# Float32r scores in row halves of the array, read two banks at a time

## The reference

```python
scores = jnp.einsum('bhqd,bhkd->bhqk', q, k) / math.sqrt(Hd)
scores = scores + causal[None, None]
attn = jax.nn.softmax(scores, axis=-1)
out = jnp.einsum('bhqk,bhkd->bhqd', attn, v)
```

## Time and profile before

| | us |
|---|---|
| median of 3 runs (782.05 to 785.3) | 783.87 |
| span of the profiled execution | 782.6 |
| stage 0 to 80: norm, first projections, first maxima | 80 |
| stage 80 to 512: maxima and scores together | 432 |
| stage 512 to 600: scores without maxima, with the work put beside them | 88 |
| stage 600 to 783: routing and experts | 183 |

### The profile page before, as it was taken

How to read it: one execution, slowest core, us unless ns; L and a number is a source line. 1 busy time by engine, 2 the same in 40 slices (tenths; PEclk the granted TensorE clock), 3 DMA queues, 4 the chain that set the end, 5 groups by cost and what they waited for, 6 DMA issues and landing times.

```text
span 782.6 us, 12208 instructions
## 1 busy us (share of the span) xinstructions
PE 689.1 (88%) x4290; PEld 367.2 (47%) x4290; DVE 561.1 (72%) x1467; ACT 459.5 (59%) x962; POOL 133.9 (17%) x194
## 2 busy tenths in 40 slices
PE   4686989999999998999999999989996279999994
PEld 3564534432323343323332323242543269999994
DVE  7754778788888787988888898960435437777762
ACT  1422445566676667766677676657783336656551
POOL 6000222220001132003310201100105300121122
PEclk9869889999999999999999999999999559999998
DMA  7436126630006033005900006000004283455200
GB/s 243 109 76 144 41 57 147 162 68 14 2 0 162 1 81 81 2 1 124 308 1 1 1 1 214 1 28 1 28 28 162 90 234 115 155 182 201 92 23 17
DMA packets 42111, 66.53 MB, mean 85 GB/s; under 512 B 3822, under 2 KB 31985, under 8 KB 41466
## 3 DMA queue, kind: packets, MB, share of 16 engines
q1 hardware_dynamic: 39746, 59.44, 27.3%
q0 software_dynamic: 2304, 6.31, 2.2%
HBM read 39.36 MB, written 26.78 MB: 85 GB/s over the span
## 4 chain that ended last, share of the span: by engine, by line
PE 74%; DVE 10%; ACT 8%; issue 4%; DMA 2%; POOL 1%; SPq 0%; DVEq 0%; POOLq 0%; ACTq 0%
PE bank L1245 17%; PE bank L1295 15%; PE bank L1325 14%; PE bank L1430 9%; PE bank L1413 8%; ACT probs L802 4%; PE bank L1187 3%; DVE chunk_max L1049 2%; PE bank L1350 2%; PE bank L1216 1%; PE bank L1396 1%; ACT qk_sb L751 1%; PE bank L1373 1%; PE bank L1228 1%; DVE stats L907 1%
## 5 line engine op out<-in xcount | busy, mean ns | idle before, releaser
L802 ACT ACTIVATE probs<-bank 128x512 f32<-128x512 f32 (+3 forms) x640 | 298.3, 537 | 124.1 <-PE bank L1325 123.0
L1049 DVE TENSOR_REDUCE chunk_max<-bank 128x1 f32<-128x512 f32 x384 | 250.7, 685 | 36.9 <-PE bank L1295 35.9
L1325 PE MATMUL bank<-stacks 104*128 104x512 bf16 (+3 forms) x640 | 195.4, 356 | 13.5 <-ACT probs L802 10.1
L1295 PE MATMUL bank<-stacks 96*128 96x512 bf16 (+3 forms) x640 | 197.7, 359 | 7.9 <-DVE chunk_max L1049 3.2
L1245 PE MATMUL bank<-probs,v_sb 128*32 128x512 f32 (+3 forms) x1280 | 151.6, 546 | 0.1
L1055 DVE CUSTOM_DVE_ANT_0 masked<-bank,causal 128x128 bf16<-128x128 f32 (+3 forms) x256 | 120.7, 484 | 15.4 <-PE bank L1295 14.6
L1295 PEld LDWEIGHTS bank<-stacks 96*128 96x128 bf16 x640 | 56.0, 98 | 160.0 <-DVE chunk_max L1049 79.4
L698 POOL TENSOR_SCALAR_AFFINE_SELECT probs<-probs 128x512 f32<-128x512 f32 x64 | 40.6, 635 | 397.4 <-ACT probs L802 397.4
L1325 PEld LDWEIGHTS bank<-stacks 104*128 104x128 bf16 x640 | 62.2, 100 | 98.7 <-ACT probs L802 65.6
L1430 PE MATMUL bank<-w_split,acts 128*128 128x256 f32 x576 | 79.9, 284 | 0.0
L1430 PEld LDWEIGHTS bank<-w_split,acts 128*128 128x128 f32 x576 | 74.5, 190 | 1.5 <-issue 0.8
(11 more groups left out here) (140 smaller groups left out, 533.6 us busy)
## 6 DMA issues: line engine op xcount, KB each, us to landing
stacks<-qk_rows SPq DMA_DIRECT2D x6, 1536.0 KB, 12.4
w_raw<-w_in SPq DMA_DIRECT2D x8, 1024.0 KB, 5.0
w_raw<-w_down SPq DMA_DIRECT2D x8, 1024.0 KB, 8.0
qk_rows<-part SPq DMA_DIRECT2D x32, 192.0 KB, 2.9
slot_rows<-empty SPq DMA_DIRECT2D x1, 5140.0 KB, 28.9
slots_sb<-slot_rows SPq DMA_DIRECT2D x8, 514.0 KB, 4.0
qk_rows<-part SPq DMA_DIRECT2D x32, 128.0 KB, 2.4
stacks<-qk_rows SPq DMA_DIRECT2D x8, 384.0 KB, 4.5
```

Of the source, the lines that this page charges most:

```text
L802: act.activation(probs[:, s % 3, h, 0:width], bank[SCORE_BANKS[u % 3]][:, 0:width], ACT.Exp)\
L1049: dve.tensor_reduce(to, src[:, 0:QB], AX.X, ALU.max).then_inc(max_read, 1)
L1295: pe.matmul(bank[MAX_BANKS[u % 3]][:, 0:width], stack(g, 0)[0:KR, h, q0:q0 + P], stack(g, 1)[0:KR, h, c * QB:c * QB + width], start=True, ...
L1325: pe.matmul(bank[SCORE_BANKS[u % 3]][:, 0:QB - lo], stack(g, 1)[0:KR + MR, h, kt * P:(kt + 1) * P], stack(g, 0)[0:KR + MR, h, b * QB + lo: ...
```

## The change

1. The parts of q and k become two float32r parts in place of three bfloat16 ones. A head takes 3 x 16 = 48 rows (high x high, high x low, low x high) and 2 more for the maxima. Two heads stand side by side in the rows of the array: one in partitions 0 to 49, one in 64 to 113.
2. A unit is now two heads: two matmuls on the two row halves, into the two banks of a pair. There are 320 units of maxima and 320 of scores. One VectorE reduction and one ScalarE exponential read both banks.
3. The three pairs of banks serve maxima and scores alike; the plan says which unit takes which pair. In the last group, once no maxima are left, the work put beside the scores has pair 0 and the scores have the other two.
4. On the diagonal, TensorE adds the mask: four matmuls of 64 columns in bfloat16 (a matrix of the large negative number by an identity) are accumulated onto the last 128 columns of the unit. The masking read on VectorE is gone.
5. The splitting is two ScalarE reads of the projection and one subtraction per block; the selector rows of L780 are gone, rows of ones are placed by four DMAs. The row of maxima goes from ScalarE through SBUF and two DMAs of SP into the stack, in place of a copy by ScalarE and one by VectorE. SP now follows the plan, so that loading of the experts comes after the last block's rows.
6. The planner is rewritten: it goes by the unit that can start first. The maxima of block 0 all use pair 0.

```diff
-PARTS_Q = [0, 0, 0, 1, 1, 2]
-PARTS_K = [0, 1, 2, 0, 1, 0]
-KR = HD * len(PARTS_Q)
-MR = 2 * HG
+HALF = P // 2
+RUNS = 3
+KR = HD * RUNS
+MR = 2
...
+        while self.maxima[self.maxed][:2] == (0, 0):
+            self.emit_max(pair=0)
...
-        MAX_BANKS, SCORE_BANKS, VALUE_BANK, MISC_BANK = (0, 1, 2), (3, 4, 5), 6, 7
+        pairs = [ctx.enter_context(nc.psum_tensor(f"pair{i}", [P, 2, QB], F32)) for i in range(3)]
...
-            return stage + (3 if t >= TAIL_TILES and t % 2 else 0)
+            if t < TAIL_TILES:
+                return stage % 2
+            return stage + (3 if t % 2 else 0)
...
-                act.copy(part[:, 0, :], qk_sb[:, :]).then_inc(part0_ready, 1)
...
-                    act.activation(stacks[KR:KR + MR, 0, 1, b, :], ones_b[KR:KR + MR, 0:1].broadcast_to([MR, S]),
-                                   ACT.Copy, scale=head_sel[KR:KR + MR, b:b + 1]).then_inc(ones_rows, 1)
...
-                    act.activation(probs[:, s % 3, h, 0:width], bank[SCORE_BANKS[u % 3]][:, 0:width], ACT.Exp)\
+                    act.activation(probs[:, s % 3, 2 * h2:2 * h2 + 2, 0:width], pairs[pair][:, :, 0:width], ACT.Exp)\
...
-                    if c < b:
-                        dve.tensor_reduce(to, src[:, 0:QB], AX.X, ALU.max).then_inc(max_read, 1)
-                        dve.tensor_tensor_reduce(out=masked[:, u % 3, 0:width], in0=src[:, 0:width],
-                                                 in1=causal[:, QB - width:QB], scale=1.0, scalar=NEG, op0=ALU.add,
-                                                 op1=ALU.max, accum_out=to).then_inc(max_read, 1)
+                    dve.tensor_reduce(chunk_max[:, n % 2, qt, :, h2, c], pairs[pair][:, :, 0:width], AX.X, ALU.max)\
+                       .then_inc(max_read, 1)
...
-                    dve.tensor_copy(rows[:, 1:HG, :], rows[:, 0:1, :].broadcast_to([MR, HG - 1, QB]))\
-                        .then_inc(max_rows, 1)
+                    sp.dma_start(stack(g, 0)[at:at + MR, :, b * QB:(b + 1) * QB].bitcast(F32),
+                                 neg_rows[hp * HG:(hp + 1) * HG, n % 2, :])\
+                      .then_inc(rows_placed[n % 2], 16)
...
-                    pe.matmul(bank[MAX_BANKS[u % 3]][:, 0:width], stack(g, 0)[0:KR, h, q0:q0 + P],
-                              stack(g, 1)[0:KR, h, c * QB:c * QB + width], start=True, stop=True).then_inc(max_scored, 1)
+                    for hp in range(2):
+                        rows = slice(hp * HALF, hp * HALF + KR)
+                        mm = pe.matmul(pairs[pair][:, hp, 0:width], stack(g, 0)[rows, h2, q0:q0 + P],
+                                       stack(g, 1)[rows, h2, c * QB:c * QB + width], start=True, stop=True)
+                    if c == b:
+
+                        for j in range(2):
+                            at = width - P + j * HALF
+                            for hp in range(2):
+                                rows = slice(hp * HALF, (hp + 1) * HALF)
+                                mm = pe.matmul(pairs[pair][:, hp, at:at + HALF], later_keys[rows, j, :],
+                                               ident_half[rows, :], start=False, stop=True, skip_group_check=True)
```

More of the change, by code:

```diff
@@ L77 @@
 PROJECT_FROM = {1: 0, 2: 1, 3: 6}
[L78 removed]
+HELD = 2
+WEIGH_AFTER = 300
 def key_tiles(b):
@@ L104 @@
               ("mods",), ("gate_bias",)]
[L107 to L140, removed]
-        width = QB if c < b else P * (qt + 1)
[L142 to L145, removed]
-            n = g * NB + b
[L148 to L165, removed]
-            return False
-        g, b, u = maxima[len(vector)]
-        if g <= block // NB:
-            return True
[L170 to L186, removed]
@@ L265, in attention_plan @@
[L265 to L273 removed]
+        if self.beside[0][0] == "turn":
+            return self.beside[0][1] < TB * through and not self.turns
+        return self.beside[0][0] != "gate" or through == NB - 1
@@ new lines, in turn_heads, with project @@
+    def turn_heads(self):
+        while self.turns and not self.piece and self.turns[0][1] <= self.now:
+            n, _ = self.turns.pop(0)
+            self.plan.append(("turn_heads", n))
+            self.now += 500
+            self.vector = max(self.vector, self.now + LATENCY) + 700
+    def project(self):
+        if not self.projections or (self.piece == 0 and self.now < self.projected + SPLIT_TIME):
+            return
+        g, b = self.projections[0]
+        if self.block() < PROJECT_FROM[g]:
+            return
+        self.plan.append(("project", g, b, self.piece))
+        self.now += 430
+        self.piece += 1
+        if self.piece == PIECES:
+            self.piece = 0
+            self.projections.pop(0)
+            self.projected = self.now
+            self.scalar = max(self.scalar, self.now + LATENCY) + 1500
+            if b == NB - 1:
+                self.parts_at[g] = self.now + SPLIT_TIME
@@ new lines, in make @@
+    def make(self):
+        while self.maxima[self.maxed][:2] == (0, 0):
+            self.emit_max(pair=0)
+        self.plan += PROLOGUE_2
+        self.now += 12000
+        while self.weighed < len(self.steps) - 1 or self.scored < 2 * len(self.steps):
+            self.turn_rows()
+            self.turn_heads()
+            found = self.choices()
+            if not found:
+                self.turn_rows(all_of=NG * NB)
+                self.now += 100
+                continue
+            at, _, emit = min(found, key=lambda c: c[:2])
+            if at > self.now + 300 or emit == self.emit_weigh:
+                self.project()
+            emit()
+        self.plan += self.beside
+        self.emit_weigh()
+        n = NG * NB - 1
+        for m, _ in self.turns:
+            self.plan.append(("turn_heads", m))
+        for k in range(TAIL_TILES, NT + TAIL_LAG + 1):
+            self.plan.extend(tail_slot(k, TAIL_TILES, NT))
+        self.plan.append(("rank", TAIL_TILES, NT))
+        self.plan.append(("gate_exp", TAIL_TILES, NT))
+        return self.plan
```

519 lines of the change are left out of this document (290 added, 229 removed).

## The result

The changed kernel takes 863.95 us (median; 862.27 to 878.01) against 782.96 for the kernel before on the same chip: ratio 1.10, interval 1.0948 to 1.1052. Forecast were 729 and a range of 690 to 790. The change makes the kernel 81 us slower. The execution of 878.01 had a clock of 0.843, the other three 0.858 or 0.859; the profile is of one of these three (863.49).

What follows compares the result with a forecast made beforehand. TensorE (85%) and VectorE (81%) were taken to set the pace together, waiting on each other in fixed order. 782.6 - 56 (stage with maxima) - 3 (stage without) + 4 (start) = 727.6, with 1.3 for the median 729; range 690 to 790.

Steps and rivals of the forecast that it cites:

- The bound of the kernel before: Stage with maxima: TensorE busy 2.74 of a 3.22 us step (85%), VectorE 2.60 (81%), waiting on each other in fixed order.
- The unit on TensorE, 0.24: Maxima and scores: a unit of two half-row matmuls costs two loads of 0.12 us; 0.183 if free, 0.37 in turn.
- Halves in turn, the slower rival: Row halves run one after the other, TensorE's step 3.43 us, total 813; chance 0.16 together with other losses.
- The mask, 0.20: Diagonal units: four mask matmuls at 0.05 us each, 0.18 a step on TensorE; bounds 0.1 and 0.5 a unit.
- VectorE, 2.60 to 2.37 a step: VectorE in the stage with maxima: fixed read cost paid 2.3 times, not 4.6; 9% less, 2.79 us at 85% use.
- The gain of 56 us: Stage with maxima: 134 steps fall from 3.22 to 2.80 us each, with TensorE at the same 85% use.
- three shared pairs are too few: Rival: hold times of the pairs set a step of 3.0 to 3.1 us, total 769 to 783; 0.19 together with late masks.
- The clock: Closing remark only: a clock granted below 1.0 in the long stage would upset the whole forecast; no size or chance given.
- The stage without maxima, -3: Stage from 512 to 600 us: eight exponentials become four, against waits on shared banks; -3 us, bounds -8 and +8.
- The start, +4: Start: chain shorter by 6 us, block 0's maxima on one pair +7, first row's DMA +3; bounds 0 and +10.
- Rows of maxima hidden by a block's steps: DMAs of later rows, asked for a block ahead, are covered by that block's steps; uncovered they would cost 37 us.
- What moved past SP: Stores, slot clearing and experts' weights behind SP's waits start some 100 us before routing, so hidden; clearing uncovered would cost 29.

Runs made afterwards that it cites:

- e3: Changed kernel with one more planner rule (cap 22): no maxima while they lead the scores by over 22 full steps; 815.65 us, ratio 1.039.
- e4: Changed kernel without the mask matmuls on TensorE, so without the causal mask of the maxima; 863.76 us, ratio 1.1002.
- e5: e3 with each exponential cut to half its columns from step 12 on; 789.52 us, ratio 1.0002.
- e6: Kernel before with each exponential cut to half its columns, as in e5; 772.56 us, ratio 0.9837.
- e14: Changed kernel with the limit on the maxima's lead at 19 full steps in place of 22; 806.13 us, ratio 1.0261.
- e10: Kernel before with matmuls of maxima and scores over rows 0 to 71, not 96 and 104; 783.7 us, ratio 0.9971.
- e2: Changed kernel with one more full-array bfloat16 matmul of 512 columns ahead of each of the 640 units; 1012.01 us.
- e8: e3 with the two DMAs of the rows of maxima issued by ScalarE behind its own copy, not by SP; 855.99 us.
- e7: Kernel before with matmuls of maxima and scores over rows 0 to 47, not 96 and 104; 1079.98 us.
- e9: Kernel before with matmuls of maxima and scores over rows 0 to 63, not 96 and 104; 868.09 and 1016.47 us.
- e15: Same program as e9, 64 rows in the kernel before, run again for its spread; 849.69 us (848.61 to 878.81).
- e11: e3 with each head's rows padded by 12 rows of zeros, to 62 for maxima and 64 for scores; 816.07 us.
- e13: Kernel before with only the matmuls of the maxima on 48 rows, scores keeping 104; 864.58 and 921.03 us.

## Why the prediction was wrong, point by point

**The bound of the kernel before**: TensorE and VectorE by waiting on each other, 85% and 81% used. This held, and the 15% was the point to take more seriously. The step of the prediction that failed is what was done with it: the use of 85% was carried over to the changed kernel, and with it came a unit priced too low, a granted clock put at no loss and a lead of the maxima that was not looked at.

**The unit on TensorE, 0.24, bounds 0.183 and 0.37.** Too high for one unit behind another, too low in the mean. Four matmuls of two units, at the full clock:

```profile
420.42 0.71 PE L1371 MATMUL pair<-stacks 50*128 50x512 f32 x4
```

Against 0.50 for one unit, the second adds 0.21: the two halves run together and the loads are hidden, the low bound. But in the timeline from 262 to 269 a unit that follows a weighing, a wait or a mask has the next instruction start 0.34, 0.34 and 0.32 us behind it (266.49 to 266.83, 268.50 to 268.84, 266.90 to 267.22): about 0.1 more, where its load stands uncovered; and 0.33 go by from the unit at 268.84 to the weighing at 269.17, where the height changes. Over the 341 units of 512 columns of e3 at the full clock with no idle time behind them, the mean is 0.34; for the mean width of 435 columns that makes about 0.31 (an estimate, 77 columns less at 0.21 / 512 us), near the 0.32 at which the prediction had TensorE's gain end. With 0.31 for the unit and 0.07 for the mask, the prediction's own sum gives 2.57 a step and at 85% 3.02: 27 us won, not 56. Halves in turn, the slower rival, did not happen: the two matmuls of a unit start 3 ns apart in the median. The rule of the Trainium skill ("TensorE: Matmul & The Clock Gate", Part 3) that two row groups start about together and loads overlap is borne out for units behind one another: 0.21 for 512 columns.

**The mask, 0.20.** It takes 0.07 (266.83 to 266.90) before the next unit starts, and in sum nothing on the path (e4).

**VectorE, 2.60 to 2.37 a step, at 85% use 2.79.** Here the working fails. Even by its own rows: 85% was TensorE's use, VectorE's was 81%, at which 2.37 gives 2.93 and a gain of 39 us. Between 200 and 400 us both kernels have the full clock (e3 has 0.97 in its second half). Before: 295 reads, 173.5 us busy and 21.1 idle before them, so two heads cost 1.18 busy and 0.14 idle, 1.32. In e3: 145 reads of two heads, 147.3 busy and 44.0 idle: 1.02 and 0.30, 1.32. These sums count records that overlap twice. By the windows, with all of VectorE's work (173.4 and 152.7 us of the 200), it is 1.18 busy before and 1.05 in e3, 10% less, near the 9% forecast, and 0.18 and 0.33 idle: what was saved came back as waiting. The windows, before and then e3, and the lines for 200 to 300:

```profile
200.00:300.00 100.00, 95.44 (x610) 35.16 (x611) 84.44 (x214) 66.83 (x149) 14.61 (x19) 1.00 0.22 51
300.00:400.00 100.00, 97.35 (x604) 32.45 (x602) 89.00 (x226) 70.38 (x152) 19.66 (x28) 1.00 0.35 98
...
200.00:300.00 100.00, 83.89 (x714) 35.78 (x716) 84.08 (x98) 64.09 (x79) 9.14 (x14) 1.00 0.23 41
300.00:400.00 100.00, 87.25 (x709) 39.85 (x710) 68.65 (x83) 64.16 (x82) 16.97 (x23) 0.97 0.24 51
```

```profile
L1049 DVE TENSOR_REDUCE chunk_max<-bank 128x1 f32<-128x512 f32 x93 | 60.7, 685 | 10.1 <-PE bank L1295 10.0
...
L1055 DVE CUSTOM_DVE_ANT_0 masked<-bank,causal 128x256 bf16<-128x256 f32 (+3 forms) x52 | 24.4, 476 | 2.5 <-PE bank L1295 2.4
```

```profile
L1095 DVE TENSOR_REDUCE chunk_max<-pair 128x2 f32<-128x1024 f32 (+3 forms) x80 | 81.4, 1060 | 15.7 <-PE pair L1343 9.6 <-PE pair L1351 5.8
```

I had carried the 85% over from six banks to three pairs. With these, a step in e3 takes 200 / 65 = 3.08 (130 exponentials of two heads), against 200 / 67 = 2.97 before (269 of one head). TensorE is busy for (83.89 + 87.25) / 65 = 2.63 of it and idle for 0.44; before it was 2.87 and 0.11. So its work fell by 0.24 a step, and its idle time grew by 0.33: TensorE, too, waits longer. The gain of 56 us is not there at all, and the rival *three shared pairs are too few*, which put the step at 3.0 to 3.1, has the step right. That the sharing is the reason is supported by e5 against e6 and by the timeline, not shown by itself; the dearer unit gives a step nearly as long. The rival's total of 769 to 783 (its upper ends add up to 786) would still have missed the time by 78 to 95 us.

**The clock.** I named it in the last sentence as what would upset all, and gave it no row, price or chance. The mean rows at work were in the diff (96 and 104 become 48 and 50), but nothing in the trace of before shows their effect; only the earlier trace rows with 0.87 at the start hints that the clock is not safe. What it costs, by an estimate: one program's executions lie apart by 23.6 us at 0.895 and 0.859 (e14), 24.3 at 0.946 and 0.906 (e10). With twice (1 - clock) times the span as time at 1.2 GHz, that is 64 and 67 us of such time, so 0.37 us lost for each. The changed kernel has 243 us at 1.2 GHz, before 89; 154 x 0.37 = 57 of the 81 lost. The price is not one number: over all programs whose executions lie 15 us or more apart it goes from 0.34 (e2) to 0.48 (the changed kernel's own, 862.27 and 878.01). So the clock's share of the 81 is some 52 to 74 us, an estimate. In the execution of 812 of e3, 168 us at 1.2 GHz are 79 more than before, by 0.37 a loss of 29: all that it lost against 784. Apart from the clock e3 is about as fast as the kernel before, and nothing of the forecast gain is left.

**The order.** The rewritten planner was looked at for block 0 only. That a longer lead starves VectorE at a group's end and delays the stacks was no rival; the wait of 22.2 is close to the 24 that are left of the 81 by the price of 0.37, though with the other prices 7 to 29 are left. Cap 22 took both: 48 = about 28 of clock (243 to 168 us at 1.2 GHz) and 20. So order and clock are not independent, and shares of the 81 beyond these sums are not shown.

**The stage without maxima, -3.** It grew by 32 (88 to 120). More steps were left for it by the long lead, and the clock is 0.93 in place of 0.98; not tested by itself.

**The start, +4.** Maxima of block 0 take from about 40.4 to 51.8 us, 11 where 13 was forecast. The busy sums to 80 are alike, but the scores begin later: the copy of the first row of maxima starts at 81.48 in place of 78.30, and the first exponential, before and after, at

```profile
80.52 0.60 ACT L802 ACTIVATE probs<-bank 128x512 f32<-128x512 f32 x1 [1.43 <-PE bank L1325]
...
90.37 1.02 ACT L847 ACTIVATE probs<-pair 128x1024 f32<-128x1024 f32 x1
```

In the 10 us between, TensorE works at 1.2 GHz on projections and maxima that the plan put first, so they are not all lost; the size is at the upper bound.

**Rows of maxima hidden by a block's steps; uncovered 15 x 2.5 = 37.** Hidden for most blocks, but where one is uncovered it lands after 9.2 us (13.9 in e3, 15.3 in e8), not 2.5, while large loads are under way; TensorE waited 8.3 for it in the stage with maxima.

**What moved past SP** stayed hidden: from the end of attention to the end of the span it takes 862 - 680 = 182 us, before 183.

Of the signs named ahead, the matmuls of a unit starting together and the reads of 1.2 us (1.23) came true, the pitch near 0.24 only for a unit between two others; the stage of 375 us and VectorE over 80% busy (335 of 480: 70%) did not; the readers idle and TensorE waiting for a pair, the sign of the rival, did.

## What to carry to other kernels

An engine used to 85% by waiting need not keep that use when its buffers and their owners change: when two readers come to share buffers, work out the hold time of each and take the step from that, not from the old percentage. Take a matmul's price from the sequence in which it will stand, with the load that nothing hides after a wait or a change of height, not from a run of equal ones. Price the granted clock as a resource of its own when a change makes matmuls shorter in rows, also if TensorE stays busy. And compare how far ahead two plans run before comparing what they run.

## What the runs showed of the hardware

- Matmuls over 48 rows, nothing else changed, bring a kernel from 786 us at a clock of 0.94 to 1068 at 0.655 and 1092 at 0.638 (e7), with TensorE busy for 49 of 50 us at 1.2 GHz; over 72 rows they cost nothing (e10); over 64 they give 849 to 1016 from one execution to another (e9, e15). Twelve rows of zeros added to each 48 left the time at 816 and the clock at 0.893 to 0.905, with 0.884 and 0.896 without them (e11, e3).
- Going over from a matmul on the whole array to one on half of its rows costs about 0.1 us (0.32 in e13, against 0.23 where both are whole, and 0.23 where both are half, in e7).
- Two float32r matmuls on the two row halves take the time of one, 0.21 us for 512 columns, with the weight loads of 0.19 hidden, if they follow another such unit; after a weighing or a wait it is 0.34.
- A DMA of the two row pairs lands 9 to 15 us after its issue while loads of stacks are under way, whichever queue it is on.
